# Attention with its key and query products on 64 rows, issued inside the score blocks, and a new order of events in a batch

## The reference

```python
xn = (inputs - mu) / jnp.sqrt(var + 1e-05) * ln_gamma + ln_beta
xh = xn.reshape(b, s, H, Dh)                     # H = 8 heads of 16
q = xh @ Wq + bq;  k = xh @ Wk + bk;  v = xh @ Wv + bv
p = pe @ Wp
content = jnp.einsum('bqhd,bkhd->bhqk', q + u_bias, k)
pos_score = _rel_shift(jnp.einsum('bqhd,khd->bhqk', q + v_bias, p))
score = (content + pos_score) / jnp.sqrt(jnp.float32(e))
attn = jax.nn.softmax(score, axis=-1)
ctx = jnp.einsum('bhqk,bkhd->bqhd', attn, v).reshape(b, s, e)
return ctx @ Wo + bo
```

## Time and profile before

| | us |
|---|---|
| device time, median of 3 runs | 553.13 |
| its runs | 553.98, 547.18, 553.13 |
| the profiled execution's own time | 551.84 |
| its span in the trace | 550.0 |
| first score matmul of step 0 | 15.11 |
| first score matmul of step 63 | 262.21 |

### The profile page before, as it was taken

How to read it: one execution, slowest core, us unless ns; L and a number is a source line. 1 busy time by engine, 2 the same in 40 slices (tenths; PEclk the granted TensorE clock), 3 DMA queues, 4 the chain that set the end, 5 groups by cost and what they waited for, 6 DMA issues and landing times. The chain is left out here.

```text
span 550.0 us, 9872 instructions
## 1 busy us (share of the span) xinstructions
PE 452.6 (82%) x3109; PEld 317.3 (58%) x3109; DVE 356.1 (65%) x893; ACT 267.4 (49%) x547; POOL 249.2 (45%) x260
## 2 busy tenths in 40 slices
PE   8798999999999999999857799738979798428870
PEld 7565666656656566666434799613454466327760
DVE  4976676676876777667434466367486566638882
ACT  2356567666666565777401355517546222025653
POOL 3452563446572862440033154442445466425771
PEclk9999999999999999999886899958989978659995
DMA  8499999999999000000040230090000000013405
GB/s 308 109 174 172 170 195 345 189 190 186 194 181 159 3 1 7 16 2 1 2 143 19 63 89 28 13 378 34 0 2 1 1 21 15 24 46 77 103 19 154
DMA packets 69395, 52.72 MB, mean 96 GB/s; under 512 B 3238, under 2 KB 67245, under 8 KB 68704
## 3 DMA queue, kind: packets, MB, share of 16 engines
q1 hardware_dynamic: 66656, 47.84, 44.0%
q0 software_dynamic: 2688, 4.25, 2.6%
HBM read 21.30 MB, written 32.09 MB: 97 GB/s over the span
## 5 line engine op out<-in xcount | busy, mean ns | idle before, releaser
L708 ACT ACTIVATE arena<-banks 128x512 f32<-128x512 f32 x128 | 76.4, 597 | 86.3 <-PE banks L921 86.1
L921 PE MATMUL banks<-ca,work 128*128 128x128 f32 x512 | 82.2, 283 | 18.2 <-ACT arena L708 14.3
L701 ACT ACTIVATE work<-banks,nmax 128x512 f32<-128x512 f32 x128 | 80.7, 686 | 13.7 <-DVE nmax L1321 13.5
L921 PEld LDWEIGHTS banks<-ca,work 128*128 128x128 f32 x512 | 53.6, 140 | 55.5 <-issue 43.0
L1321 DVE TENSOR_REDUCE nmax<-banks 128x2 f32<-128x1024 f32 x64 | 78.3, 1224 | 2.2
L903 PE MATMUL banks<-arena 32*128 32x512 f32 (+3 forms) x256 | 60.1, 435 | 0.0
L892 PEld LDWEIGHTS banks<-arena 32*128 32x128 f32 x256 | 41.2, 184 | 30.4 <-issue 23.2
L892 PE MATMUL banks<-arena 32*128 32x128 f32 x256 | 55.2, 295 | 0.6 <-DVE corr L1401 0.6
L1309 DVE COPY_PREDICATED banks<-ca,banks 128x256 f32<-128x256 uint32 x64 | 27.2, 426 | 38.1 <-PE banks L892 37.9
L1046 PE MATMUL banks<-t,arena 128*128 128x128 f32 x300 | 47.1, 295 | 3.9 <-ACT t L815 1.0
L1101 PE MATMUL banks<-arena 128*128 128x512 f32 x96 | 45.4, 623 | 1.2 <-POOL arena L680 1.2
(11 more groups left out here) (221 smaller groups left out, 828.9 us busy)
## 6 DMA issues: line engine op xcount, KB each, us to landing
regions<-zeros SPq DMA_DIRECT2D x15, 1040.0 KB, 18.4
regions<-zeros SPq DMA_DIRECT2D x9, 1032.0 KB, 19.9
arena<-wp_in SPq DMA_DIRECT2D x1, 4624.0 KB, 26.3
arena<-wp_in SPq DMA_DIRECT2D x1, 4494.0 KB, 15.9
arena<-ct_in SPq DMA_DIRECT2D x2, 1024.0 KB, 9.7
arena<-regions SPq DMA_DIRECT2D x29, 65.0 KB, 1.9
arena<-cb_in SPq DMA_DIRECT2D x1, 1660.0 KB, 8.2
arena<-regions SPq DMA_DIRECT2D x23, 64.5 KB, 1.9
```

The source lines that it names most:

```text
L701: eng.activation(prob[:, r, :], bank[r], ACT.Exp, bias=nmax[:, s % 2, jj:jj + 1]).then_inc(s_exp, 1)
L708: eng.activation(probT[:, v % 2, j0 + jj, :, i % 2 * P:(i % 2 + 1) * P], PT.rearrange("p (t q) -> p t q", t=TB), ACT.Copy).then_inc(s_pTs, 1)
L921: mm = eng.transpose(PT[:, t * P:(t + 1) * P], prob[:, 2 * (s % 2) + jj, t * P:(t + 1) * P], ident)
```

## The change

`k`, `t1` and `t2` read only the 64 rows of their group, from the weights and from `xnT` alike: `product(k)`. 21 of these 24 products (all but those ahead of step 0) are no longer jobs of their own on PE. A new `ride(s, ...)` puts them into score s + 2, between `before(1)` and `before(0)`, and only where the group is the one whose 64 rows that step's pair doesn't use (the assertion). On the other engines the events of `ride(s)` stand behind score s + 2, where those of `at(s)` stand ahead of it. The order of events inside a batch is written anew.

```diff
+    def ride(step, *events):
+        assert events[0][-1] == (step + 1) % 2
+        behind.setdefault(step, []).extend(events)
...
-        at(base + 11, ("job", "t2", b, 1), ("q", b, 1))
-        at(base + 13, ("job", "v", b), ("xbo", b))
+        at(base + mid + 11, ("job", "v", b), ("xbo", b))
+        ride(base + mid + 12, ("job", "t2", b, 1), ("q", b, 1))
...
         if s + 2 < STEPS:
             plan.append(("score", s + 2))
+            for e in behind.pop(s, []):
+                put(e)
+                if e[0] == "job":
+                    riders[s + 2] = len(jobs) - 1
...
+            def product(k):
+
+                name, b, g = jobs[k]
+                rows, part = slice(g * P // NG, (g + 1) * P // NG), queries(name)
+                eng.wait_ge(*after("zT", b))
+                if name == "k":
+                    eng.wait_ge(s_ca[1], 16)
+                    weights = A(f"wk{g}", rows)
+                else:
+                    eng.wait_ge(*after("fold", 0))
+                    n = 2 * g + (name[1] == "2")
+                    weights = wt[rows, n * P:(n + 1) * P]
+                return eng.matmul(job_bank[k][:, part], weights, xnT[rows, part], start=True, stop=True)
...
                     diagonal(0).then_inc(s_d0, 1)
                     before(1)
+                    if s in riders:
+                        bank_free(riders[s])
+                        product(riders[s]).then_inc(s_job, 1)
                     before(0)
                     behind(1)
                     behind(0)
```

More of the change, by code:

```diff
@@ L90, in plan_attention @@
     per = NG * 2 * TB
-    later = {}
+    later, behind, riders = {}, {}, {}
     def at(step, *events):
         later.setdefault(step, []).extend(events)
+    def ride(step, *events):
+        assert events[0][-1] == (step + 1) % 2
+        behind.setdefault(step, []).extend(events)
     for e in (("stats", 0), ("cols", 0), ("kd", 0), ("job", "pem", 0), ("job", "wqT", 0), ("normz", 0), ("job", "bias", 0),
@@ L102, in plan_attention @@
         put(("delta", 0, i))
[L103 to L106, removed]
+    ride(0, ("job", "k", 0, 1), ("kb", 0, 1))
+    at(1, ("job", "v", 0))
+    ride(2, ("job", "t1", 0, 1))
+    at(3, ("xbo", 0))
+    ride(4, ("job", "t2", 0, 1), ("q", 0, 1))
     at(16, ("job", "wo", 0))
@@ L110, in plan_attention @@
         base = per * (b - 1)
-        first = 3 if b == 1 else 0
+        first = 4 if b == 1 else 0
+        mid = 2 if b == 1 else 0
         at(base if b == 1 else base - 1, ("stats", b))
@@ L114, in plan_attention @@
         at(base + first + 1, ("job", "zT", b))
[L115 to L120, removed]
-        at(base + 11, ("job", "t2", b, 1), ("q", b, 1))
-        at(base + 13, ("job", "v", b), ("xbo", b))
+        ride(base + first + 2, ("job", "k", b, 1), ("kb", b, 1))
+        ride(base + first + 3, ("job", "k", b, 0), ("kb", b, 0))
+        ride(base + mid + 7, ("job", "t1", b, 0))
+        at(base + mid + 8, ("job", "corr", b))
+        ride(base + mid + 9, ("job", "t2", b, 0), ("q", b, 0))
+        ride(base + mid + 10, ("job", "t1", b, 1))
+        at(base + mid + 11, ("job", "v", b), ("xbo", b))
+        ride(base + mid + 12, ("job", "t2", b, 1), ("q", b, 1))
     for m in range(1, B * NG):
@@ L127, in plan_attention @@
         base = per * b
-        at(base + 12, ("job", "ctxT", 2 * b))
+        at(base + (13 if b else 15), ("job", "ctxT", 2 * b))
         at(base + 20, ("job", "ctxT", 2 * b + 1))
@@ L154, in plan_attention @@
             plan.append(("score", s + 2))
-    assert not later, later
-    return jobs, plan
+            for e in behind.pop(s, []):
+                put(e)
+                if e[0] == "job":
+                    riders[s + 2] = len(jobs) - 1
+    assert not later and not behind, (later, behind)
+    return jobs, plan, riders
 def plan_recurrence():
@@ L176, in build @@
 def build(nc, x_in, ca_in, ct_in, cb_in, wp0_in, wp1_in, out):
-    jobs, plan = plan_attention()
+    jobs, plan, riders = plan_attention()
     number = {j: k for k, j in enumerate(jobs)}
@@ L870, in _, with bank_free @@
             used = {}
+            def product(k):
[10 more added lines that the diff above has]
+                return eng.matmul(job_bank[k][:, part], weights, xnT[rows, part], start=True, stop=True)
+            def bank_free(k):
+                at_bank = next(n for n in range(8) if bank[n] is (early[jobs[k][0]] if k < n_early else JOB))
+                if at_bank in used:
+                    eng.wait_ge(*done[used[at_bank]])
+                used[at_bank] = k
             for kind, *w in plan:
@@ L939, in _ @@
                     mm.then_inc(s_pv, 1)
-                elif kind == "job":
+                elif kind == "job" and w[0] not in riders.values():
                     k = w[0]
@@ L943, in _ @@
                     bk = job_bank[k]
[L944 to L948, removed]
+                    bank_free(k)
                     if name == "pem":
@@ L973, in _ @@
                             mm = eng.transpose(bk[:, t * P:(t + 1) * P], z[:, t, :], ident)
[L974 to L977, removed]
                     elif name == "v":
@@ L983, in _ @@
                                             start=True, stop=True)
[L984 to L990, removed]
+                    elif name == "k" or name[0] == "t":
+                        mm = product(k)
                     elif name == "corr":
```

## The result

The changed kernel takes 621.33 us in the median of six runs (611.29 to 633.11) where the kernel before takes 551.11. Half of its runs, and some of the runs further down, are disturbed ones with a lower clock; ratios leave them out, and here the ratio is 1.112, with a 95% interval of 1.104 to 1.120. So it is slower, as predicted, but by far more: the profiled execution has 611.29 us where the forecast was 568 and the range ended at 597. Score 63 starts at 326.65 us, where before it started at 262.21 and where I expected about 277. So +64.4 us inside attention is to be explained, of which the prediction had 15.3. Behind score 63 the profiled execution takes 611.29 - 326.65 = 284.6 us, before 551.84 - 262.21 = 289.6.

What follows compares the result with a forecast made beforehand. The prediction took PE, in a circle with ACT, to bound attention. It summed -17.0 + 19.4 + 7.8 + 3.1 + 2 = +15.3 us on 551.84 to 567, 568 as the median, with a range of 557 to 597.

Steps and rivals of the forecast that it cites:

- products out of the way: In attention's steps, 21 products no longer stand ahead of scores on PE, 0.81 us each: -17.0 us.
- bank 7: PE waits for DVE's later readout of the product: 13 x 1.1 + 6 x 0.85 = +19.4 us.
- single t1: Readout of t1(b,1) must wait for POOL's q(b,0): 2.6 us in batches 1, 2 and 3, +7.8 us.
- z of batch 2: PE's zT(2) waits for POOL's z, which comes behind q(1,1), rstd: +3.1 us.
- the clock: Half clock behind four long PE waits (three q, one z): 0 to 7 us, taken as +2 us.
- Does the product hide in the score?: Inside a score, the 64-row product streams in idle rows beside the 32-row blocks and costs nothing.
- the other end: Upper bound for a product inside a score: the whole product in line with the rest.
- the rival: PE drains between 64-row and 32-row blocks in scores: 1.5 us for each of 18 products, 27; total 590; chance 0.38.
- T + 4.39: T is a product-carrying score's start; if the next score carries one too, it stops behind its first blocks until then.

Runs made afterwards that it cites:

- 32-row kernel, busy PE: 32-row kernel plus PE products of 256 columns whose results go unused, ahead of jobs PE waits for; ratio 1.031, median 565.0 us.
- 32-row kernel: Changed kernel, but its 21 products inside scores read 32 of their 64 rows, half of each sum left out; ratio 1.076, median 603.59 us.
- useless products: Unused 256-column PE products ahead of jobs PE waits for; added to the 32-row kernel 1.031, to the changed kernel 1.099, with fitted numbers 1.081.
- the early readout: 32-row kernel, second t1 tile, unused products only ahead of zT(2); DVE reads the product out before the score's maximum, not behind; ratio 0.988, 553.79 us.

## Why the prediction was wrong

By the sum's own terms, for the 64.4 us that score 63 came later:

| | predicted | shown |
|---|---|---|
| products out of the way, bank 7, single t1, z of batch 2 | 13.3 | 15.2 (32-row kernel, busy PE) |
| the product in line with its score | 0 | about 27 (15 products at 1.28, times 21) |
| the clock | 2 | about 22 (what is left), some 4 of it at the start, behind no wait |

**"Does the product hide in the score?": the step that failed.** I took nothing, because the nearest row was the pair's own heads running side by side, and left the other end to a rival. The nearest row had blocks of one shape. It couldn't speak for a block of another, and the same trace had rows in which the shape changed, each time at 0.21 us, which I read as getting in and out. Three runs settle it. At the same place in the score, 32 x 128 hides in full (the transposes 1.28 us behind the score's start). 64 x 128, 128 x 128 and 32 x 64 are served alone, and the transposes come 2.49 to 2.96 us behind its start (full clock, bank free). The Trainium skill says in TensorEngine Tiling (Array Packing), Tiling Modes, that a change of mode drains the engine and a change of tile doesn't. The traces agree, for rows and for columns. I had quoted it, given 0.38 to its result, and priced it rightly: 1.5 us for each of 18 products, 27 in all. Its working holds tile by tile. 1.28 + 0.86 + 2 x 0.21 and the lost overlap make 2.77, 2.56, 2.77 and 2.99 us for query tile 0 to 3; the changed kernel has 2.74, 2.54, 2.74 and 2.96 (scores 25, 27, 13 and 6).

**"The clock": the second step that failed, by its size.** I had the cause, that waits with PE idle bring a stretch at half clock, but took the only row that I had, 3.41 us behind attention, for the size of each. In attention the five stretches behind waits were 6.8 to 23.9 us long, and 54.5 us together. In them the transposes come 2.44 us behind a score's start (1.28 at full clock), with a product 5.16. The 22 us are a remainder, 64.4 - 15.2 - 27, and rest on a cross-check: in the 32-row kernel the useless products took 78.6 us at half clock away (82.0 less 3.4) and gained 27.3, a third. A third of 54.5 is some 18, and with the 4 of the start, which no wait explains and no term of the sum covers, that is the 22. Neither the forecast nor the rival had this, so even the rival ended at 600, below the 611.29.

**The rest held.** Bank 7: the single wait is 1.12 us against 1.1, and the early readout gave back 13.7 us (some 1 of it the clock's, and less what the later maximum costs) against 15.3 for the 15 products. In step 21 above the product waits until 105.23, and the prediction's T + 4.39, from score 20 at 100.83, is 105.22. The single t1: 2.55 against 2.6. z of batch 2: step 18 takes 7.03 us in the 32-row kernel with a busy PE and 3.72 would be a step with four transposes, so 3.3 against 3.1. In the changed kernel it is this row, and the long stretch at half clock begins right behind it:

```profile
112.64 3.12 POOL L575 TENSOR_SCALAR z<-xa,mv,rstd 128x128 f32<-128x128 f32 x4 [0.18 <-POOL rstd L549]
...
115.90 0.82 PE L1004 MATMUL banks<-ca,z 128*128 128x128 f32 x4 [3.11 <-POOL z L575]
```

That products leave the path by 0.81 us each is right as well, but only for a shape that this change doesn't use. The 13.3 and the 15.2 agree as sums of terms of both signs; the 2 us between them I can't assign.

**The chances.** Slower had 0.77, which was right. Within it I should not have put the forecast above the rival: the rule that I had from the Trainium skill spoke for the rival, and no row spoke against it. The range ended at 597 because the clock stood in every case with 7 us at most: the rival's 590 with 22 for it instead of 2 is 610.

## What to carry to other kernels

Before you count on idle rows, compare the shape of the block (rows x columns) with those that it is to run beside: only an equal shape runs beside them here, and any other stands in line with its whole length. If work is moved into another engine's shadow, move its readout too, since the old place of the readout decides when the bank comes free. And price a new wait of PE with what the clock does behind it: here some 18 us in the changed kernel and 27 in the 32-row one, beside waits that the prediction priced at 30.

## What the runs showed of the hardware that I had not expected

- Three blocks of equal shape on rows of their own run at once: the 32 x 128 product began 0.01 us behind the score's first block (32.72 and 32.71), and the score took no longer for it.
- Put between 32 x 128 blocks, a 64 x 128 product that takes 1.05 us from its start to the next block's (80.12 to 81.17) makes the step 1.2 to 1.7 us longer at full clock (4.53 for 3.33 and 6.66 for 4.99 in steps 27 and 30 of the kernels with useless products). One change ahead of a job costs 0.19 us (4.33 for 4.14).
- A wait of 3.11 us, in a stretch of 4.20 us with 0.93 us of PE work, was followed by 23.9 us at half clock in which PE was busy throughout. Being busy didn't bring the clock back at once.
- The clock also fell without a wait: at 13.8 us, behind 6.80 us in which PE was busy throughout, for 13.7 us. Six of the thirteen profiled executions have such a stretch beginning between 13.4 and 15.9 us; the one with products over 128 rows, otherwise the same kernel, has none. What decides it stays open.
- Useless products made a kernel faster: 100 more MATMULs, and score 63 27.3 us earlier, because the clock stayed at 2.4 GHz.
